# A linear-attention block on one core: VectorE evicts two heads, ScalarE two whose mask TensorE adds, and GpSimd takes over routing steps and the row normalising

## What is computed

```
x = x + linear_attention(layernorm(x))     # causal, 16 heads of 8, phi = elu + 1
x = x + experts(layernorm(x))              # 16 experts, 4 per token, 2 shared ones
x = x + softmax_attention(layernorm(x))    # 16 heads of 8, over 256 tokens
x = x + experts(layernorm(x))
```

## Time and profile before

| | us |
|---|---|
| median of 3 runs | 578.68 |
| lowest, highest | 577.07, 580.25 |
| the profiled execution | 574.57 |
| its span in the profile | 572.8 |
| first attention, first product to second unit | 15.8 to 116.3 |
| busy: TensorE | 517.6 |
| busy: VectorE | 432.7 |
| busy: ScalarE | 344.8 |
| busy: GpSimd | 290.0 |

### The profile page before, as it was taken

The page is one execution under the profiler, slowest core; times in us unless marked ns, Lnnn a source line. Parts: engine busy times, 40 slices in busy tenths (PEclk is TensorE's granted clock), DMA queues, the critical chain, the costliest instruction groups (busy, mean ns, idle before and its releaser), DMA issues. The chain is left out here.

```text
span 572.8 us, 11532 instructions
## 1 busy us (share of the span) xinstructions
PE 517.6 (90%) x3757; PEld 390.4 (68%) x3757; DVE 432.7 (76%) x1105; ACT 344.8 (60%) x607; POOL 290.0 (51%) x276
## 2 busy tenths in 40 slices
PE   3878887899999999999788898988999999999996
PEld 3555564577888888888454555645678888888884
DVE  3678798569798898567677887989479796886663
ACT  3676746456555655666457767676865655555553
POOL 4765572146666756777421305020166656666664
PEclk9799988899999999999779999999999999999999
DMA  6358870213454344235641524310442444354340
GB/s 168 114 185 263 245 249 2 72 62 98 107 116 127 92 119 121 98 112 180 200 117 51 185 75 143 116 39 3 62 106 97 109 135 124 103 137 132 95 143 20
DMA packets 48549, 67.60 MB, mean 118 GB/s; under 512 B 6625, under 2 KB 18930, under 8 KB 48498
## 3 DMA queue, kind: packets, MB, share of 16 engines
q1 hardware_dynamic: 45392, 66.47, 39.9%
q10 hardware_dynamic: 3106, 0.48, 0.5%
HBM read 53.56 MB, written 13.37 MB: 117 GB/s over the span
## 5 line engine op out<-in xcount | busy, mean ns | idle before, releaser
L639 POOL TENSOR_TENSOR KS<-PT,QS 128x512 fp32r<-128x512 f32 x144 | 186.2, 1294 | 118.1 <-ACT QS L836 106.1
L831 ACT ACTIVATE bank<-bank 128x512 f32<-128x512 f32 x128 | 74.5, 582 | 98.5 <-PE bank L856 97.9
L1562 DVE TENSOR_TENSOR PT<-CS,bank 128x512 f32<-128x512 f32 x128 | 87.4, 683 | 45.1 <-PE bank L856 44.3
L854 PE MATMUL bank<-XH,WH 128*128 128x512 f32 (+1 forms) x288 | 115.4, 401 | 1.7 <-DVE PT L1434 1.5
L856 PE MATMUL bank<-XH,WL 128*128 128x512 f32 (+1 forms) x288 | 112.9, 392 | 0.0
L855 PE MATMUL bank<-XL,WH 128*128 128x512 f32 (+1 forms) x288 | 112.6, 391 | 0.0
L836 ACT ACTIVATE QS<-PT 128x512 fp32r<-128x512 f32 x144 | 90.1, 626 | 12.2 <-DVE PT L1567 11.8
L1458 DVE TENSOR_REDUCE MEXP<-bank 128x4 f32<-128x1024 f32 x64 | 78.2, 1223 | 22.8 <-PE bank L966 22.1
L1567 DVE TENSOR_TENSOR PT<-PT,bank 128x512 f32<-128x512 f32 x128 | 88.0, 687 | 9.5 <-ACT bank L831 1.6
L750 ACT ACTIVATE PT<-bank 128x1024 f32<-128x1024 f32 x64 | 65.6, 1025 | 40.1 <-PE bank L998 39.8
L1021 PE MATMUL bank<-PT,V 128*32 128x256 f32 (+1 forms) x1024 | 64.6, 372 | 0.3 <-ACT OTS L760 0.3
(11 more groups left out here) (185 smaller groups left out, 770.6 us busy)
## 6 DMA issues: line engine op xcount, KB each, us to landing
CS<-combine_rows SPq DMA_DIRECT2D x128, 256.0 KB, 3.2
head_rows<-HP SPq DMA_DIRECT2D x28, 256.0 KB, 3.0
QS<-head_rows SPq DMA_DIRECT2D x28, 256.0 KB, 2.7
KS<-head_rows SPq DMA_DIRECT2D x28, 256.0 KB, 3.0
head_rows<-PHI SPq DMA_DIRECT2D x14, 256.0 KB, 3.1
out_dram<-X SPq DMA_DIRECT2D x4, 256.0 KB, 3.7
stage<-in_L_ffn_gate_w_dram SPq DMA_DIRECT2D x5, 192.0 KB, 3.8
stage<-in_L_ffn_up_w_dram SPq DMA_DIRECT2D x5, 192.0 KB, 4.0
```

Of the source, the lines that this page charges most:

```text
L639: pool.tensor_tensor(GL[:, (u - 1) % 3, :], GG[:, (u - 1) % 3, :], GH[:, (u - 1) % 3, :].bitcast(f32), ALU.subtract).then_inc(F.gl, 1)
L831: act.activation(TH[:, u, :] if u < SHARED else G[u % 3][:, :], G[u % 3][:, :], ACT.Silu).then_inc(F.th, 1)
L854: pe.matmul(out, wh, vh, start=start, stop=False)
L1562: dve.tensor_tensor(ab, CS[:, e % CBUFS, :], U[u % 3][:, :], ALU.mult).then_inc(F.b, 1)
```

## The change

In the first attention each head's bank is now laid out as diagonal, diagonal, full. VectorE takes all three blocks of heads 0 and 1 in one operation (`first_heads`, a mask of 384 columns), ScalarE all three of heads 2 and 3 in one (`last_heads`, with Relu). For heads 2 and 3 TensorE adds, behind the products, a matrix that is 0 where the score stays and -2^126 where it has to vanish: a matmul of the identity with `BELOW`, 256 columns, accumulated into the bank. VectorE makes both operands in slot 2. The products of heads 0 and 1 wait for VectorE, those of heads 2 and 3 for ScalarE.

GpSimd makes the normalised rows itself (`normalise`), where a shift on GpSimd and four operations on ScalarE did it. Of the routing, GpSimd takes the arithmetic, VectorE keeps max, match and the sums; the best two of a group are now found by 16 max operations. The first feed-forward unit comes one slot later in both layer pairs, the weight pieces move by up to one slot and behind the eviction on ScalarE.

```
-        PIECE_SLOTS = [9, 11, 16, 18, 24, 26]
+        PIECE_SLOTS = [9, 11, 15, 17, 23, 25]
+        POOL_ROUTE_SLOTS = [{24: (0,), 25: (2,), 27: (3,), 29: (5,), 30: (7,)},
+                            {27: (0,), 28: (2,), 29: (3,), 31: (5,), 32: (7,)}]
+        DVE_ROUTE_SLOTS = [{25: (1,), 26: (2, 3), 28: (4, 5), 30: (6,)},
+                           {28: (1,), 29: (2, 3), 30: (4, 5), 32: (6,)}]
...
-        UNIT_SLOT = [35, 36]
+        UNIT_SLOT = [36, 37]
-        LATE_SLOTS = [{1: (35, 36), 2: (37,), ...
+        LATE_SLOTS = [{1: (36,), 2: (37,), ...
...
+            def normalise(L, c):
                 norm_pool(L, c)
                 pool.wait_ge(L.rs, c + 1)
-                pool.tensor_tensor(RM[:, :], MV[:, :, 0], RS[:, :], ALU.mult).then_inc(L.nb, 1)
-                pool.wait_ge(L.nb, 2 * c + 1)
-                pool.tensor_tensor(NB[:, :], RM[:, :], NEG[:, :], ALU.mult).then_inc(L.nb, 1)
+                if c:
+                    pool.wait_ge(L.xt, c)
+                for t in range(CT):
+                    i = pool.tensor_scalar(XN[:, t, :], X[:, c * CT + t, :], MV[:, t, 0:1], RS[:, t:t + 1],
+                                           ALU.subtract, ALU.mult)
+                i.then_inc(L.xn, 1)
...
+                if part == 3:
+                    after(7)
+                    pool.tensor_tensor(pool_junk[:, :], NEG[:, 0:1], NEG[:, 0:1], ALU.mult)
+                    link(8, pool.tensor_scalar(GMK[:, :, :], GR[:, :, 0:GROUPS], -BIG / 3, None, ALU.is_lt))
...
-                    act.activation(PT[:, i % 2, 2 * x:2 * x + 2, P:2 * P], S4[:, 2 * x:2 * x + 2, P:2 * P], ACT.Copy)\
-                       .then_inc(A.fb, 1)
+                def last_heads(i):
+                    act.wait_ge(A.s1, 4 * i + 4)
+                    if i >= 2:
+                        act.wait_ge(A.pv, i - 1)
+                    act.activation(PT[:, i % 2, 2:4, 0:3 * P], S4[:, 2:4, 0:3 * P], ACT.Relu).then_inc(A.fb, 1)
...
                         if i and h == 0:
-                            pe.wait_ge(A.fb, 2 * i)
+                            pe.wait_ge(A.mk, i)
                         if i and h == 2:
-                            pe.wait_ge(A.mk, 2 * i)
-                        pe.matmul(S[h][:, 0:SEQ], keys[r, j, k0:k0 + P], queries[r, q0:q0 + SEQ], start=True, stop=True)
-                        pe.matmul(S[h][:, SEQ:SEQ + P], keys[r, j, k0 + P:k0 + SEQ], queries[r, q0 + P:q0 + SEQ],
-                                  start=True, stop=True).then_inc(A.s1, 1)
+                            pe.wait_ge(A.fb, i)
+                        pe.matmul(S[h][:, P:P + SEQ], keys[r, j, k0:k0 + P], queries[r, q0:q0 + SEQ], start=True, stop=True)
+                        m = pe.matmul(S[h][:, 0:P], keys[r, j, k0 + P:k0 + SEQ], queries[r, q0 + P:q0 + SEQ],
+                                      start=h < 2, stop=True, skip_group_check=h >= 2)
+                        if h >= 2:
+                            m = pe.matmul(S[h][:, 0:SEQ], ident_r, BELOW, start=False, stop=True, skip_group_check=True)
+                        m.then_inc(A.s1, 1)
...
+                def first_heads(i):
+                    dve.wait_ge(A.s1, 4 * i + 2)
+                    if i >= 2:
+                        dve.wait_ge(A.pv, i - 1)
+                    dve.tensor_tensor(PT[:, i % 2, 0:2, 0:3 * P], S4[:, 0:2, 0:3 * P],
+                                      MASK.unsqueeze(1).broadcast_to([P, 2, 3 * P]), ALU.mult).then_inc(A.mk, 1)
```

More of the change, by code:

```diff
@@ L269, in hybrid_block @@
         s_out = sem("stored")
-        LN = [NormSems(sem, f"ln{k}_", k != 2) for k in range(4)]
+        LN = [NormSems(sem, f"ln{k}_", k == 0) for k in range(4)]
         s_rows_read = [sem(f"head_rows{j}_loaded") for j in range(4)]
@@ L602, in slot @@
                         route_constants()
+                    if n == ITEMS + 4:
+                        pool.wait_ge(A.mk, ITEMS)
+                        pool.memset(MEXP[:, :, :, :], 0.0)
                     if n == 2:
@@ L630, in slot @@
                                        ALU.subtract).then_inc(Lnext.xl, 1)
+                for part in POOL_ROUTE_SLOTS[k].get(n, ()):
+                    route(A, 0, part)
             def unit(k, c, u, cur, prev, more):
@@ L651, in unit @@
                                        ALU.subtract).then_inc(LN[2].xl, 1)
+                if more:
+                    for part in POOL_ROUTE_AT[prev].get(u, ()):
+                        route(AT[k], c + 1, part)
             layers(pool, slot, unit)
@@ L1328, in after @@
                     dve.wait_ge(A.rv, base + k)
-                sbi4 = SBI[:, :, :].rearrange("p t (g i j) -> p (t g) i j", i=2, j=2)
-                if part == 0:
+                if part == 1:
                     dve.wait_ge(s_pc, 9)
[L1333 to L1342, removed]
-                    link(3, dve.tensor_tensor(PMN[:, :, :], sbi4[:, :, :, 0], sbi4[:, :, :, 1], ALU.min))
                     after(3)
-                    dve.tensor_tensor(T1[:, :], PMX[:, :, 0], PMX[:, :, 1], ALU.max)
-                    dve.tensor_tensor(T2[:, :], PMX[:, :, 0], PMX[:, :, 1], ALU.min)
-                    link(4, dve.tensor_tensor(T3[:, :], PMN[:, :, 0], PMN[:, :, 1], ALU.max))
+                    dve.memset(route_junk[:, :], 0.0)
+                    for t in range(CT * GROUPS):
+                        i = dve.max(out=TOP[:, t, :], in_=SB8[:, t, :])
+                    link(4, i)
                 if part == 2:
-                    after(4)
-                    link(5, dve.tensor_tensor(T2[:, :], T2[:, :], T3[:, :], ALU.max))
                     after(5)
-                    link(6, dve.tensor_tensor(GE[:, :, 0:GROUPS], T1[:, :].rearrange("p (t g) -> p t g", g=GROUPS),
-                                              T2[:, :].rearrange("p (t g) -> p t g", g=GROUPS), ALU.add))
+                    dve.memset(route_junk[:, :], 0.0)
+                    for t in range(CT):
+                        i = dve.max(out=GM[:, t, :], in_=GE[:, t, :])
+                    link(6, i)
+                if part == 3:
                     after(6)
@@ L1510, in side_steps @@
                         norm_aggregate(Lnext, c - 2)
-                    for part in ROUTE_SLOTS[k].get(n, ()):
+                    for part in DVE_ROUTE_SLOTS[k].get(n, ()):
                         route(A, 0, part)
@@ L1532, in slot @@
                     if n == 2:
+                        below()
                         bias_rows()
@@ L1580, in unit @@
                 if more:
-                    for part in ROUTE_AT[prev].get(u, ()):
+                    for part in DVE_ROUTE_AT[prev].get(u, ()):
                         route(AT[k], c + 1, part)
```

193 lines of the change are left out of this document (97 added, 96 removed).

## The result

The changed kernel takes 598.8 us (median of four, 595.8 to 613.8) against 578.1 us. The ratio is 1.035, 95% interval 1.030 to 1.041; a second measurement gave 1.034 (1.029 to 1.039). The change makes the kernel 3.5% slower, where the prediction had 1.9% (589.6 us, range 571 to 597). The direction was right, the size about half, and the time lies 1.8 us above the range. Ratios leave out slow executions, over 1.5% above a kernel's fastest; the changed kernel with its rows on ScalarE had three in four and then five in seven of them, so its times count for little.

A forecast was written before the change was run, and what follows sets the result against it. TensorE bounds the kernel, with 18.2 us idle in the first attention. +10.0 + 7.5 - 4.0 - 2.6 = +10.9 us takes the profiled 574.57 to 585.5, the median to 589.6 us; range 571 to 597.

The forecast's parts named there:

- Product step: TensorE, first attention: products with mask passes take 1.36 us an item, 1.0 more than before; 1.5 more in first chunk.
- The streaming rival: TensorE between products: mask passes stream without drains, 0.44 us an item, -9.2 us to 569.5; chance 0.18.
- Eviction: First attention: VectorE's two operations become one of 0.95 us, ScalarE's two one of 0.81; waits covered except at item 1.
- The 1.2 us that item 1 was to wait: First attention: slot 3 has no values product, so item 1 waits about 1.2 us for ScalarE's eviction.
- First piece: First attention, items 0 to 8: mask passes and waits lengthen 27.9 us to 38.3; +10.0 us taken.
- Second piece: First attention, items 9 to 30: two estimates, +8.4 and +6.7 us, with slow-clock stretches gone in the first; +7.5 taken.
- Third piece: Item 31 and feed-forward start: slot 35 and earlier rows fill TensorE's waits, 9.66 becomes 5.6 us, -4.0.
- The first attention in all: First attention: the three pieces together, +10.0, +7.5 and -4.0 us.
- Row normalising: GpSimd's four operations at 0.4 us replace ScalarE's; rows ready 0.6 us earlier, TensorE waits less, -2.6 us together.
- the rival "GpSimd": GpSimd's scalar operations cost 1.02 us each, rows come 4.1 us after the power instead of 2.0: 596 us; chance 0.12.
- Routing: Routing shared by GpSimd and VectorE: links lie a slot or unit apart, waits covered; 0 us, -1 to +1.
- the part on the moved queue: GpSimd's queue: lower halves, bias row and new routing steps stand behind the rows; the wait for earlier transposes is long met.

The follow-up runs named there:

- mask last, alone: The kernel before with only the new eviction and the mask passes behind all four heads, routing and slots unchanged: 575.5 us, ratio 0.994.
- the fastest kernel: The changed kernel with mask passes behind all four heads, rows on ScalarE, first feed-forward routing links one unit later: 571.1 us, 0.988 of the kernel before.

## Why the prediction was right in the first attention and short behind it

*Product step: right.* 1.36 us was said, 1.29 to 1.38 measured; in the first chunk 2.34 for 2.38. The sum of head time, mask stream, load and switch held. The Trainium skill ("TensorEngine Tiling (Array Packing)", section "Key Properties") says that a change of tiling mode drains TensorE. The trace agrees: a mask pass stands 0.31 us ahead of the next product where a pure stream is 0.12. By the order of instructions each item got two more changes of mode (three where the values product follows), not the four more that the prediction counted; its sum prices two. Leaving the row groups once instead of twice per item made the largest difference of the study, two thirds of it because head 3 runs beside the others again. The streaming rival fell at once.

*Eviction: right.* 0.954 and 0.812 us for 0.95 and 0.81. The 1.2 us that item 1 was to wait never appeared: TensorE was at half clock there, so one item's products lasted 4.2 us (16.84 to 21.04 us in its timeline) and covered it.

*First piece: +10.0 said, +11.5 measured, and +1.0 ahead of it* (first product at 16.84 for 15.81 us, the mask operands), of which 0.55 was in the +10. I put the excess down to the clock: these lines of the changed kernel are the same operations as above at double length, up to 29 us.

```profile
18.96 1.22 PE L1011 MATMUL bank<-PQ,CS 32*128 32x256 f32 x2
20.53 0.58 PE L1015 MATMUL bank<-Q 128*128 128x256 f32 x1
```

The second profile of before has such a start as well (doubled up to 25 us), so this belongs to the execution more than to the change.

*Second piece: +7.5 said, +4.65 measured* (67.56 for 62.91 us). The direct sum of steps, +6.7, was nearer, and the two slow stretches that were in it before are gone. I had taken the middle between that sum and busy time plus steps, +8.4, which was the worse of the two.

*Third piece: -4.0 said, -3.2 measured.* The rows kept 0.8 of it.

*The first attention in all: +13.5 said, +14.0 in the first pair of profiles.* A second pair gives +11.2 (turn 7 at 128.12 for 116.97 us). So this half of the working holds, to some 2 us; that +13.5 and +14.0 are so close is partly luck, since 2.5 us too little for the start and the first piece, 2.9 too much for the second and 0.8 too little for the third cancel.

*Row normalising: this step failed.* It said: "I take 0.4, near the one-input row", "the rows are then ready some 0.6 us earlier", "never queued behind ScalarE's evictions", -2.6 us. An operation measures 0.80 us, so the four last 3.14 us where ScalarE's last 1.65 and the two small ones 0.5: ready 1.0 us later, not earlier, which is the +1.0 us at turn 8. The compare over 128 elements at 0.29 us was a poor neighbour: it was the nearest in width, not in form, for the new one has two operands of one value per partition. That the form makes the difference is likely and was not tested. The upper bound of 1.02 us was nearer, and the rival "GpSimd" was priced for just this, at 593 to 600 us. The measured time lies in its range partly by luck: the rows alone are 1.0 us at turn 8 and +0.1% in time, and the rest came from the routing, the clock and what stays open below. Its sum is also off: 589.6 + 2.6 + 4 x 1.8 is 599.4 us, not 598. The Trainium skill ("GPSIMD Engine Reference", section "Elementwise — side-by-side cycle accounting") puts the body of a short operation at 1.03 cycles an element, 0.11 us for 128 elements as an estimate, and names a dispatch of each instruction beside it without a figure for GpSimd. The measured 0.80 us is seven times that estimate and decides. Set against 0.4 it would have been 1.2 us for four, not the 0.8 of the prediction.

*Routing: right alone, wrong in this kernel.* "I take 0": alone it is 1.000. But the part on the moved queue listed what stands behind the rows, and not what stands ahead of them. A link that waits for VectorE holds GpSimd for 1.20 us with the statistics behind it: +1.7 us at turn 8, of which 1.4 go with the links one unit later.

*The account.* From turn 7 to the last matmul the changed kernel takes 462.5 and 460.3 us in two profiles, the kernel before 453.2 and 455.0: +7.3 us on the mean, where the prediction had a gain. 2.7 us are the later rows of the last chunk, shown above. 1.6 to 2.7 us are the half clock at the end of that wait (8 to 9 is 57.5 and 58.7 for 55.9 us). The rest, about 2.4 us, lies in the second attention and behind; from turn 11 to the end (267 us before) the changed kernel takes 305.9 and 304.9 us, the kernel before 302.1 and 303.9, and mask last, alone, which changes nothing there, 305.5. So I can't give it to the change. TensorE waits there 1.9 and 2.5 us for the rows where it waited 0.9 and 0.8, which is one of its parts; the fastest kernel, with its rows on ScalarE, waits 2.5 us there too, so that part is not GpSimd's rows alone. The second profile of the kernel before was taken to see whose the difference is: 453 to 454 us from turn 7 on would have made all of it the change's, 455 to 457 us some 3 us of it the first execution's. It is 455.0, 1.8 us above the first.

The spans differ by 23.2 us and the medians by 20.7, because the first profile of before was a quick execution, 3.5 us below its median, and that of the changed kernel is 0.9 below. The miss is 20.7 - 10.9 = 9.8 us: 7.3 behind turn 7 and the 2.6 of a gain that didn't come. Of the 7.3 us, some 5 have a place and 2.4 have none.

## What to carry to other kernels

Count the changes between row groups and the whole array, and the heads that no longer run side by side, not the columns: the same two mask passes cost 4.0% (24 us by the medians) between the heads and 0.7% (4 to 6 us) behind them. Before work moves to another engine's queue, list what stands ahead of it there, waits included, and price the operation by its form and operands, not by its width alone. A gain that stands on an operation the trace doesn't show should be taken from the pessimistic neighbour, above all where its result is the last thing TensorE waits for.

## What the runs showed of the hardware

GpSimd's tensor_scalar with two operands of one value per partition takes 0.80 us for 128x128 in fp32; GpSimd's tensor_tensor over 64 columns takes 0.29, and over 512 columns 1.28. The same rows take ScalarE 0.48.

In four of the five profiles with a wait of 3.3 us at turn 8 a half-clock stretch began within 1.3 us of the end of the wait, on either side of it. With waits of 2.3 us or less there was none in eleven profiles, and one in three, all of kernels with the masks between the heads (profiles of 602, 612 and 626 us). That is what stood together in time, not a tested cause.

The time until TensorE first runs at full clock varies between executions of one kernel: up to 10.7 and 25.4 us from the start in two profiles of the kernel before, and 76 us in two profiles of changed kernels (612 and 626 us). In those two, turn 7 came at 149 and 159 us instead of 130. It was not for lack of work: in the first of them TensorE is busy for 46.00 us of the 46 from 30 to 76 us, with a product step of 4.07 us where 2.34 is the full-clock one. The trace has no record of the clock up to there, and the column for it reads 1.00.
